# Set-up of a graph layer: loads in another order with several semaphores, the tally first on TensorE, the edge ranges passed through DRAM during the first pass

## What is computed

```python
xn = _layernorm(x)                                   # 6250 x 512
h = xn @ W.T; e_src = h @ a_src; e_dst = h @ a_dst
e = leaky_relu(e_src[src] + e_dst[dst])              # 100000 edges, dst sorted, plus a loop on each node
alpha = segment_softmax(e, dst)
gnn = xn + elu(segment_sum(alpha[:, None] * h[src], dst) + bias)
q, k, v = relu(q), relu(k), v of xn @ Wqkv.T         # 8 heads of 64
mix = (q @ (k.T @ v) * temperature / clip(q . sum(k), 100)) @ Wproj.T + bproj
x = x + gnn + mix
x = x + moe_top2_of_8(_layernorm(x))                 # 512 -> 256 -> 512, layer norm in each expert
```

## Time and profile before

| | us |
|---|---|
| median of 3 runs | 2688.14 |
| lowest and highest | 2682.47 and 2689.73 |
| time of the profiled execution | 2689.04 |
| its span in the trace | 2687.3 |
| end of the loads, first instruction of VectorE | 24.69 |
| first load of the first pass issued | 46.98 |
| TensorE without a pause from | 61.60 |
| end of the first pass's block | 290.24 |

### The profile page before, as it was taken

The page is one execution under the profiler, slowest core; times in us unless marked ns, Lnnn a source line. Parts: engine busy times, 40 slices in busy tenths (PEclk is TensorE's granted clock), DMA queues, the critical chain, the costliest instruction groups (busy, mean ns, idle before and its releaser), DMA issues. The chain is left out here.

```text
span 2687.3 us, 53608 instructions
## 1 busy us (share of the span) xinstructions
PE 2450.9 (91%) x12032; PEld 1387.6 (52%) x12033; DVE 1624.5 (60%) x4117; ACT 902.2 (34%) x1583; POOL 1283.5 (48%) x1272
## 2 busy tenths in 40 slices
PE   3999899999999889999999999999999639999995
PEld 2555577766666423333444444444444326777773
DVE  2655466664222244466666666666667575889886
ACT  0333344442111100011122222323333426677774
POOL 1444520000000477777776666555545154777774
PEclk9999899999999899999999999999999759999998
DMA  4333733331001477777777776666666355777775
GB/s 177 127 128 123 97 110 101 103 103 33 24 24 32 129 207 213 211 219 227 243 241 224 217 212 207 206 207 197 197 193 205 137 192 102 130 131 132 132 129 82
DMA packets 178069, 409.96 MB, mean 153 GB/s; under 512 B 46749, under 2 KB 46781, under 8 KB 176930
## 3 DMA queue, kind: packets, MB, share of 16 engines
q0 software_dynamic: 90512, 280.63, 40.0%
q1 hardware_dynamic: 59074, 76.65, 10.3%
q10 hardware_dynamic: 28368, 51.41, 5.6%
HBM read 339.65 MB, written 68.82 MB: 152 GB/s over the span
## 5 line engine op out<-in xcount | busy, mean ns | idle before, releaser
L1056 POOL DMA_INDIRECT rows<-h_rows,src_col x784 | 783.8, 1000 | 481.4 <-PE acc_ps L1159 228.8
L1159 PE MATMUL acc_ps<-rows,W 128*128 x1776 | 838.8, 611 | 59.1 <-DVE W L1257 33.2
L1159 PEld LDWEIGHTS acc_ps<-rows,W 128*128 128x128 f32 x1776 | 310.9, 190 | 527.0 <-issue 526.4
L1257 DVE TENSOR_SCALAR W<-window,dst_col,w_col 128x128 f32<-128x128 f32 x888 | 300.3, 372 | 314.5 <-PE acc_ps L1159 263.5
L1635 POOL DMA_INDIRECT out<-y,idx_add x105 | 168.5, 1605 | 112.4 <-issue 47.1
L649 POOL DMA_DIRECT2D alpha_d<-score x1 | 0.6, 573 | 461.8 <-DVE score L967 461.8
L1085 ACT ACTIVATE a_sd<-a_mv,cst 128x1 f32<-128x1 f32 x49 | 14.4, 295 | 606.6 <-DVE a_mv L1323 606.6
L1679 PE MATMUL o_ps<-w,hidT 128*128 x420 | 202.7, 605 | 7.4 <-DVE z L1739 3.2
L1669 PE MATMUL hid_ps<-xsT,w_now 128*128 128x128 f32 x1680 | 206.7, 277 | 0.2 <-issue 0.2
L1669 PEld LDWEIGHTS hid_ps<-xsT,w_now 128*128 128x128 f32 x1680 | 197.8, 194 | 1.0 <-issue 1.0
L773 PEld LDWEIGHTS q_ps<-hxnT,wqkv 128*128 128x128 f32 x1568 | 182.4, 193 | 11.9 <-issue 11.9
(11 more groups left out here) (303 smaller groups left out, 3470.2 us busy)
## 6 DMA issues: line engine op xcount, KB each, us to landing
lo_row<-src_lo SPq DMA_DIRECT2D x98, 256.0 KB, 3.3
xb<-in_x SPq DMA_DIRECT2D x49, 256.0 KB, 2.7
h_rows<-kb SPq DMA_DIRECT2D x49, 256.0 KB
fold_w<-in_x SPq DMA_DIRECT2D x49, 256.0 KB
rows<-h_rows,src_col POOLq DMA_INDIRECT x784, 3.8
a_own<-h_rows ACTq DMA_DIRECT2D x49, 256.0 KB, 3.8
a_xr<-in_x ACTq DMA_DIRECT2D x49, 256.0 KB, 5.2
out<-a_x ACTq DMA_DIRECT2D x49, 256.0 KB, 4.7
```

The costliest lines, as they stand in the source:

```text
L1056: nc.gpsimd.indirect_dma_start(G[:, n % ROWS, :], None, h_rows, bass.IndirectOffsetOnAxis(ap=src_col[:, n:n + 1], axis=0)).then_inc(row_in ...
L1159: nc.tensor.matmul(acc_ps[s][:], W[:, j, :], G[:, ds(row, 1), :].rearrange("p o d -> p (o d)"), start=(opens and j == 0), stop=(j == VT - ...
L1257: nc.vector.tensor_scalar(W[:, j, :], window[:], dst_col[:, ds(at_tile + j, 1)], w_col[:, ds(at_tile + j, 1)], ALU.is_equal, ALU.mult).the ...
```

## The change

The loads are asked for in another order and raise five semaphores in place of one: first `last_col` and the constants (`first_in`), then the four edge arrays that VectorE works on and `dst_last` (`loaded`, 80 for five of them), then `avec` and `w_nat` (`u_in`), then `wg` (`wg_in`). The zeroes of `starts_d` come next, then `temp`, `src_col` and `wqkv` (`wqkv_in`), and then, as before, `src_lo` once `ints` is 2. SP's block ends when `src_lo` and the zeroes have landed; TensorE waits for `wg_in` at its first product with `wg` in the first pass, and SP for `wqkv_in` at that pass's end.

VectorE begins at `first_in` 32 and waits for `loaded` 80 once the one-hot matrices are made. TensorE does the tally's matmuls and the two products behind it, then the 32 matmuls of `u`, then those of the ranges.

The write of `ranges_d` moves into SP's stream of the first pass, behind the load of tile 3; the wait for it and the read into `ranges` stand behind the load of tile 5; `ranges` is waited for at the end of the pass. For that `rout_i` (16 bytes in a partition) now lives as long as the tensors of the passes over the nodes, and lies in front of `u` and `wg`.

```diff
@@ -232,6 +232,8 @@
+            rout_i = sb(sc, "rout_i", [NT, 4], I32)
+            first_in, u_in, wg_in, wqkv_in, r_saved, r_loaded = (sem(n) for n in ("first_in", "u_in", "wg_in", "wqkv_in", "range_saved", "range_loaded"))
@@ -252,11 +254,9 @@
-            rout_i = sb(ps, "rout_i", [NT, 4], I32)
-            r_loaded = sem("range_loaded")
@@ -270,21 +270,21 @@
-                        for dst, src in ((cst[:], a["consts"]), (wg[:], a["wg"]), (w_nat[:], a["w_nat"]),
-                                         (wqkv[:], a["wqkv"]), (avec[:], a["avec"]),
-                                         (temp[:], a["temp"]), (src_col[:], a["src_col"]),
-                                         (dst_i[:], a["dst_col"]), (lin_i[:], a["src_lin"]), (src_row[:], a["src_row"]),
-                                         (dst_row[:], a["dst_row"]), (last_i, a["last_col"]), (last_bc[:], a["dst_last"].partition_broadcast(NT))):
+                        for dst, src in ((last_i, a["last_col"]), (cst[:], a["consts"])):
+                            sp.dma_start(dst, src).then_inc(first_in, 16)
+                        for dst, src in ((lin_i[:], a["src_lin"]), (src_row[:], a["src_row"]), (dst_i[:], a["dst_col"]),
+                                         (dst_row[:], a["dst_row"]), (last_bc[:], a["dst_last"].partition_broadcast(NT))):
                             sp.dma_start(dst, src).then_inc(loaded, 16)
+                        sp.dma_start(avec[:], a["avec"]).then_inc(u_in, 16)
+                        sp.dma_start(w_nat[:], a["w_nat"]).then_inc(u_in, 16)
+                        sp.dma_start(wg[:], a["wg"]).then_inc(wg_in, 16)
                         sp.wait_ge(nothing_ready, 1)
                         sp.dma_start(starts_d[0:EP, :].rearrange("(p e) k -> p (e k)", p=P), nothing).then_inc(zero_out, 16)
+                        for dst, src in ((temp[:], a["temp"]), (src_col[:], a["src_col"]), (wqkv[:], a["wqkv"])):
+                            sp.dma_start(dst, src).then_inc(wqkv_in, 16)
                         sp.wait_ge(ints, 2)
                         sp.dma_start(src_lo.rearrange("(p c) -> p c", p=LC), lin_lo[:]).then_inc(saved, 16)
-                        sp.wait_ge(ints, 18)
-                        sp.dma_start(ranges_d, rout_i[:, 0:2]).then_inc(saved, 16)
-                        sp.wait_ge(saved, 32)
-                        sp.dma_start(ranges[:], ranges_d.rearrange("(o t) c -> o (t c)", o=1)).then_inc(r_loaded, 16)
-                        sp.wait_ge(r_loaded, 16)
+                        sp.wait_ge(saved, 16)
                         sp.wait_ge(zero_out, 16)
@@ -294,13 +294,6 @@
-                        pe.wait_ge(loaded, 208)
-
-                        for k in range(KC):
-                            for j in range(KC):
-                                last = nc.tensor.matmul(u_ps[:, 2 * k:2 * k + 2], w_nat[:, j, k * P:(k + 1) * P],
-                                                        avec[:, j, :], start=(j == 0), stop=(j == KC - 1))
-                        last.then_inc(u_done, 1)
@@ -308,6 +301,12 @@
+                        pe.wait_ge(u_in, 32)
+                        for k in range(KC):
+                            for j in range(KC):
+                                last = nc.tensor.matmul(u_ps[:, 2 * k:2 * k + 2], w_nat[:, j, k * P:(k + 1) * P],
+                                                        avec[:, j, :], start=(j == 0), stop=(j == KC - 1))
+                        last.then_inc(u_done, 1)
                         pe.wait_ge(ints, 14)
@@ -318,7 +317,7 @@
-                        dve.wait_ge(loaded, 208)
+                        dve.wait_ge(first_in, 32)
@@ -328,6 +327,7 @@
+                        dve.wait_ge(loaded, 80)
                         step.done(nc.vector.tensor_scalar(lin_i[:], lin_i[:], P - 1, None, ALU.bitwise_and))
@@ -421,7 +421,11 @@
                                 sp.dma_start(xb[s][:], a["x"][ds(t * P, P), :]).then_inc(x_in[s], 16)
+                                if isinstance(t, int) and t == XR + 1:
+                                    sp.wait_ge(r_saved, 16)
+                                    sp.dma_start(ranges[:], ranges_d.rearrange("(o t) c -> o (t c)", o=1)).then_inc(r_loaded, 16)
                                 if isinstance(t, int) and t == XR - 1:
+                                    sp.dma_start(ranges_d, rout_i[:, 0:2]).then_inc(r_saved, 16)
                                     sp.dma_start(gbias, a["gbias"].partition_broadcast(P)).then_inc(g_in, 16)
@@ -429,6 +433,8 @@
+                        sp.wait_ge(r_loaded, 16)
+                        sp.wait_ge(wqkv_in, 48)
@@ -496,6 +502,8 @@
+                                if isinstance(t, int) and t == 0:
+                                    pe.wait_ge(wg_in, 16)
```

## The result

| | before | changed |
|---|---|---|
| median of 7 runs, us | 2688.14 | 2669.95 |
| lowest and highest | 2682.47 to 2691.84 | 2663.53 to 2675.66 |
| ratio to before, with its 95% interval | | 0.9933 (0.9918 to 0.9948) |
| span of the profiled execution | 2687.3 | 2669.1 |
| first `xb` issued | 46.98 | 28.30 |

The changed kernel is 0.67% faster. The forecast was 2669. In the trace the first pass starts 18.7 us earlier and ends 19.2 us earlier; what follows it takes 2398.1 us where it took 2397.1.

A forecast was written before the change was run, and what follows sets the result against it. Set-up was taken as two serial stretches, loads then computing, delaying a TensorE-bound first pass; overlapping them until the DMA queue ends starts the pass 19.3 us earlier: 2688.14 - 19.3 = 2668.8, said as 2669, range 2662 to 2677.

The forecast's parts named there:

- What bounds the kernel: Set-up: 24.69 us of loads without computing, then 22.29 us with DMA 6% busy; from 61.60 us TensorE sets the pace.
- the sum: Whole kernel: median 2688.14 less 19.3 us of set-up gives 2668.8, with everything behind set-up keeping its length.
- The tally's chain: Set-up computing: VectorE begins at about 6.1 us, five arrays land at 10.3, computing ends at 23.9 instead of 43.26.
- the slack that I put at 14 us: Set-up loads: the arrays VectorE needs could land as late as 14 us at no cost.
- What ends set-up: SP's DMA queue: `src_lo` behind `wqkv` lands at 27.1; first `xb` at 27.7 instead of 46.98, 19.3 us less.
- The ranges: First pass, SP: the moved write and read cost nothing; their two set-up waits, 2.4 and 2.1 us, are in the 19.3.
- The long issues: Set-up, SP: if 4.55 us is `last_col`'s own price, all lands 4.5 us later: 14.8 us less, 2673; 10%.
- The queue's order: Set-up loads: unordered service delays VectorE's arrays, 8.3 us less, 2680, 4%; or `src_lo` passes `wqkv`, 2666, 5%.
- The placement: Passes over the nodes: tensors moved by 16 bytes are read more slowly, 15 us over before, 2703; 3%.
- Giving back: Behind set-up: a wait behind the pass or a lower clock takes 5 to 11 us, about 2677; 5%.
- the estimate by that page: Set-up loads: at about 358 GB/s 9.42 MB take 26.3 us; pass starts at 29.3, 17.7 us less.

The follow-up runs named there:

- The edit with `src_lo` ahead: The changed kernel with `wqkv` asked for behind `src_lo` instead of ahead of it: ratio 0.9922 to the kernel before, first `xb` at 25.04 us.
- the ranges in set-up: The changed kernel with the write of the ranges, its wait and the read back in set-up: ratio 0.9945 to the kernel before, first `xb` at 32.98 us.

## Why the prediction was right, by its steps

*What bounds the kernel.* Right. That everything behind set-up would keep its length was the step on which the sum stood; the first pass took 242.7 us from its first load where it took 243.3, and the rest 1.0 us more.

*The tally's chain.* Right in form, 0.7 us off at its end: `used_by` ended at 24.61, forecast 23.9. VectorE began at 6.21 (6.1). The term that was off is the landing of the five arrays, 12.0 in place of 10.3; the rate that I carried over from the earlier trace rows is that of other loads, and this queue ran at some 300 GB/s between 6 and 8 us. (By the earlier trace rows itself the 2.76 MB had passed at 8.7 us and not at my 9.0, and the slack that I put at 14 us is 10.3 + 3.2 = 13.5; neither is in the sum.) TensorE began `u` at 15.46 for 14.2, and VectorE's wait for it was 2.02 us for 2.8. The chain was covered with 3 us to spare, so none of this reached the time.

*What ends set-up.* Right: `src_lo` lands last and the computing is over 3.7 us before. The size was 0.6 us short, 28.30 for 27.7, and that is two errors that partly cancel. The bytes ran out slowly: 168 GB/s over the last 3.69 us, the last of them at about 27.15, where my terms put it at 25.8. And the 1.3 us from last byte to landing were misread: I had let the last of the 9.22 MB pass at 25.3 at 427 GB/s, but the trace of before, cut more finely, has 31 GB/s still between 25.8 and 26.0, so its zeroes landed 0.6 us behind the last traffic, as `src_lo` did 0.5 us behind it in the changed kernel. The edit with `src_lo` ahead shows that this tail, and not the computing, was the bound.

*The ranges.* Their part of the sum was right in what it said of the changed kernel: at 41.46 the read is issued without a wait worth noting, and SP's list of waits has none for `ranges_d`. My reading that a write in a busy queue lands with the queue was wrong for the ranges, as the ranges in set-up showed: 4.7 us and not 2.4. The prediction used it only for `src_lo`, where it held. It also counted the two waits with 4.5 us within its 19.3; by itself, in the kernel before, this part brings 3.3.

*The rivals.* The long issues were queueing: 0.42 us for `last_col` on an empty queue, and 5.13 us for another small load once `wqkv` stood in front. The queue's order held: 7.0 us for 3.15 MB, and `src_lo` did not pass `wqkv`. The placement costs nothing that the trace shows: L508 took 609 ns each and L500 before 610. Giving back: 1.0 us in the trace, within what the stretch behind the pass varies by. The rate of some 358 GB/s, which the Trainium skill gives as the limit with device memory (DMA: Bandwidth & Descriptors, "Where 436 GB/s comes from"), is passed here for long: the changed kernel moved 406 GB/s over 18.40 us. The start came at 28.30, between my 27.7 and the 29.3 of the estimate by that page, for another reason: fast loads and a slow tail.

*The range.* 2662 to 2677 held the median and all seven runs. That the median lies within 1 us of the forecast is in part luck: the seven runs spread over 12 us, and the first pass ended 19.2 us earlier while the rest took 1.0 us more. What bears the mechanism out is the marks in the trace.

## What to carry to other kernels

A set-up in which the DMA engines are full while no engine computes, and then the reverse, has at most as much to give as the shorter of the two; ask for the loads in the order of need, give each consumer its own semaphore, and then read what lands last: here it was the queue's tail. Before a large load is moved to where "nobody waits for it", look at every transfer on the same DMA engines, another engine's small gathers above all: here they turned 3.6 us of an earlier start into 1.4 us lost. Parts of such a change don't add up: undone one at a time, the three cost 15.1, 5.6 and 4.7 us of a gain of 18.7, and the last one alone in the old kernel is worth 3.3.

## What I had not expected of the hardware

- A DMA's long issue said nothing of that DMA. With the 3.15 MB load fourth in the queue, the twelfth and thirteenth issues took 4.55 and 3.65 us; with it third, the thirteenth took 5.13; with it last, all fourteen took 0.34 to 0.69 us.
- A tiny write into a busy queue wasn't done when the queue was: 392 bytes landed 2.6 us after the last traffic (1.8 when they moved alone), while 196 KB of `src_lo` landed about 0.5 us after it. I don't know what sets the two apart; that one goes in rows of 8 bytes was not tried apart.
- Two gathers from Pool's queue took 9.6 and 9.1 us beside the 3.15 MB of SP's queue, for 2.8 or 2.9 in the undisturbed pass. The Trainium skill (DMA: Bandwidth & Descriptors, "Queues, rings and completion order") has each DMA engine alternate between its queues packet by packet; by that I would have expected a small gather to get through early. The load landed at 39.6 and the first of the two gathers at 35.8, so it did not wait for all of it, only for most. Why, no run shows.
